# One setup block at the start and the state-space beginning inside the last attention batch of a four-layer conditioned sequence kernel

## The reference, cut to what matters

```python
# L0: 16 heads of 16, gelu MLP (no silu before the modulation)
h = ln(x) * (1 + scale) + shift        # scale, shift = split(cond @ Wln1 + bln1)
x = x + attention(h);  x = x + mlp(ln(x) * (1 + scale2) + shift2)
# L1: 16 heads of 64, L2: 16 heads of 16 with a padding mask; both gated
mod = silu(cond) @ W_mod + b_mod       # shift, scale, gate for attention and for MLP
x = x + gate * attention(modulate(ln(x), ...));  x = x + gate2 * mlp(modulate(ln(x), ...))
# L3: state space in both directions, then a gated MLP
h = ln(x, w, b) * (1 + s1) + sh1
def mamba(h):
    x, z = split(h @ in_proj_W)                    # 512 + 512 channels
    x = silu(causal_conv4(x) + conv_b)
    dt, B, C = from(x @ x_proj_W)                  # dt = softplus(... @ dt_proj_W + dt_proj_b)
    hst = hst * exp(dt * A) + dt * B * x           # 32 states per channel, 512 steps
    return (sum(hst * C) + Dp * x) * silu(z) @ out_proj_W
x = x + g1 * (mamba(h) + flip(mamba(flip(h))))
x = x + g2 * (silu(h2 @ w1) * (h2 @ w2)) @ w3
```

## Time and profile before

| | us |
|---|---|
| runs | 6488.37, 6493.69, 6502.44 |
| median | 6493.69 |
| profiled execution, its own time | 6495.14 |
| its span in the trace | 6493.1 |

### The profile page before, as it was taken

How to read it: one execution, slowest core, us unless ns; L and a number is a source line. 1 busy time by engine, 2 the same in 40 slices (tenths; PEclk the granted TensorE clock), 3 DMA queues, 4 the chain that set the end, 5 groups by cost and what they waited for, 6 DMA issues and landing times. The chain is left out here.

```text
span 6493.1 us, 77727 instructions
## 1 busy us (share of the span) xinstructions
PE 5849.5 (90%) x28624; PEld 3037.7 (47%) x28624; DVE 4492.7 (69%) x4945; ACT 4210.7 (65%) x6876; POOL 2659.1 (41%) x1962
## 2 busy tenths in 40 slices
PE   6989899999999998998997888989899888888887
PEld 3444445555555554444443444444444444444444
DVE  4565663344444345656654898989899898989897
ACT  2444344444555443443443998989898998989896
POOL 0000002222222222000000695959597795959596
PEclk8999999999999999999998999999999999999999
DMA  4221320000000001223131101010110201011100
GB/s 113 51 39 32 58 49 22 1 1 1 1 1 1 1 1 37 50 39 55 32 57 24 53 27 50 30 47 30 42 33 19 58 25 52 30 47 30 47 30 18
DMA packets 152634, 216.11 MB, mean 33 GB/s; under 512 B 24193, under 2 KB 91033, under 8 KB 151745
## 3 DMA queue, kind: packets, MB, share of 16 engines
q1 hardware_dynamic: 152112, 211.08, 14.0%
q10 hardware_dynamic: 144, 0.07, 0.0%
HBM read 146.54 MB, written 30.44 MB: 27 GB/s over the span
## 5 line engine op out<-in xcount | busy, mean ns | idle before, releaser
L2192 DVE TENSOR_TENSOR_SCAN l__h<-l__decay,psum 128x1024 f32<-128x1024 f32 x1024 | 2276.9, 2271 | 74.2 <-ACT l__decay L1800 29.2
L2176 POOL TENSOR_TENSOR l__hc<-l__h,l__c_rep 128x1024 f32<-128x1024 f32 x1024 | 2037.9, 2003 | 186.9 <-DVE l__h L2192 140.4
L1807 PEld LDWEIGHTS psum<-ident,l__dtx_B 128*128 128x128 f32 x8192 | 889.7, 142 | 1102.8 <-DVE l__h L2192 684.9
L1807 PE MATMUL psum<-ident,l__dtx_B 128*128 128x128 f32 x8192 | 1129.9, 282 | 260.7 <-ACT l__dtx_B L1785 185.0
L1800 ACT ACTIVATE l__decay<-l__dt_rep,l__a_neg 128x511 f32<-128x511 f32 x2048 | 1353.4, 712 | 14.9 <-DVE l__h L2192 14.8
L1785 ACT ACTIVATE l__dtx_B<-l__dtx_T,l__b_T 128x512 f32<-128x512 f32 x1792 | 1197.9, 713 | 37.9 <-PEq L2285 35.8
L2261 PE MATMUL psum<-l__hc,l__gather 128*64 128x512 f32 x4096 | 1112.6, 622 | 12.3 <-POOL l__hc L2176 11.7
L192 POOL TENSOR_SCALAR l__ln_var_eps<-l__ln_mean_var 128x4 f32<-128x4 f32 x64 | 17.5, 274 | 2292.2 <-DVE l__ln_mean_var L178 2291.6
L657 DVE TENSOR_REDUCE l__row_max<-psum 128x1 f32<-128x512 f32 x1024 | 658.4, 687 | 250.0 <-PE psum L672 248.8
L1294 POOL TENSOR_SCALAR l__probs<-l__probs,l__rec 128x512 f32<-128x512 f32 x512 | 349.9, 696 | 967.9 <-DVE l__rec L1290 967.8
L966 ACT ACTIVATE l__probs<-psum 128x1024 f32<-128x1024 f32 x512 | 515.6, 1025 | 280.1 <-PE psum L1027 275.7
(11 more groups left out here) (165 smaller groups left out, 6973.1 us busy)
## 6 DMA issues: line engine op xcount, KB each, us to landing
l__c_rep<-l__c_dram SPq DMA_DIRECT2D x512, 128.0 KB, 2.8
l__dt_rep<-l__dt SPq DMA_DIRECT2D x128, 256.0 KB, 4.8
l__parts_dram<-l__parts SPq DMA_DIRECT2D x64, 384.0 KB, 3.8
l__q_stack<-l__parts_dram SPq DMA_DIRECT2D x192, 128.0 KB, 6.4
l__k_stack<-l__parts_dram SPq DMA_DIRECT2D x192, 128.0 KB, 9.1
l__w<-in_l_w SPq DMA_DIRECT2D x6, 1024.0 KB, 7.5
mod_w<-in_mod_w SPq DMA_DIRECT2D x2, 2816.0 KB, 12.5
x_sb<-in_x SPq DMA_DIRECT2D x1, 4096.0 KB, 27.2
```

The lines of the kernel that those rows point to most:

```text
L1807: last = nc.tensor.transpose(bx_psum(i)[:, s, t * P:(t + 1) * P], dtx_B[:, k % 2, t, 2 * c + s, :, :].rearrange("p j d -> p (j d)"), ident ...
L2176: nc.gpsimd.tensor_tensor(hc[:, i % HCS, :, :], h[:, i % HS, :, :], c_of_i, ALU.mult).then_inc(S["hc"], 1)
L2192: nc.vector.tensor_tensor_scan(both(h[:, i % HS, :, :]), both(decay[:, i % DECAYS, :, :]), both(bx_psum(i)), 0.0, ALU.mult, ALU.add).then_ ...
```

## The change

**At the start.** The setup is a class, `Modulation`, and its work stands in the same block as L0's beginning, `alone(setup)`, so one block and one barrier are gone. The columns are in two parts: FIRST (0 to 7, 1024 columns of weights) and REST (8 to 43, 4608). `x` comes in three DMAs: batch 0, batch 1, batches 2 to 7. The mask rows are written, and waited for, after all loads are issued, and L0's stack DMAs (`first_sync`) stand behind that wait on SP.

**At the beginning of L3.** `mamba_layer` returns a `First` and a body. `body2(first3)` hosts batch 0's beginning in L2's last batch, and two blocks (weights, beginning) are gone. ACT takes the four in-projected columns (`take_x`) ahead of `l__hT_mlp`; DVE does the taps (`convolve`) during the MLP; PE projects four of eight in-columns behind the out projection and the rest after the last residual. The memsets of `xproj` and `dtw` are on POOL, `l__a_neg` is made in two steps on ACT. `wout`, `w1`, `w2` and `w3` are loaded in the first batch's block of L3 (`late_sync`). L3's tiles are placed by hand at other addresses (`REGIONS3`), and the two halves of `l__dtx_B` change places. The barrier after L2's last batch clears 120 semaphores where it cleared 60.

```diff
-        alone0()
+        alone0(setup)
         body0(first1)
         body1(first2)
-        body2(None)
+        body2(first3)
+        body3()
 
# alone(setup): sync, vector (parts), tensor
+                    setup.load_first(sp)
                     load(sp)
+                    setup.load_rest(sp)
+                    setup.masks_out(sp)
                     first_sync(sp)
...
-                    ahead.vector(nc, dve, 0, 0)
+                    dve.wait_ge(setup.s_x[0], 16)
+                    norm.stats(nc, dve, ahead.of(0), 0)
+                    setup.mask_rows(dve)
+                    setup.first_columns(dve)
+                    ahead.take_columns(nc, dve, 0)
+                    ahead.scaled(nc, dve, 0, 0)
                     first_vector_stats(dve)
                     first_vector_scaled(dve)
+                    dve.wait_ge(setup.s_x[1], 16)
                     second_vector(dve)
                     first_vector_down(dve)
+                    setup.rest_columns(dve)
+                    dve.wait_ge(setup.s_x[2], 16)
...
+                    for m in setup.FIRST:
+                        setup.fill(pe, m)
+                    pe.wait_ge(setup.s_consts, 4)
                     norm.tensor(nc, pe, 0, bank[0:DC])
                     first_tensor_project(pe)
                     first_tensor_norm(pe)
                     second_tensor(pe)
+                    rest = iter(setup.REST)
+                    for _ in range(len(setup.REST) - LEAD // 3):
+                        setup.fill(pe, next(rest))
                     first_tensor_down(pe)
                     for n in range(LEAD):
                         first_tensor_step(pe, n)
+                        if n % 3 == 2:
+                            setup.fill(pe, next(rest))
                     first_tensor_end(pe)
...
# Modulation.load_first / load_rest / masks_out
+        self.load_w(sp, 0)
+        self.load_x(sp, 0)
+        sp.dma_start(self.bias[:, :], self.io["mod_b"]).then_inc(self.s_in, 16)
+        sp.dma_start(self.nw[:, :], self.io["norm_w"]).then_inc(self.s_in, 16)
+        sp.dma_start(self.nb[:, :], self.io["norm_b"]).then_inc(self.s_in, 16)
+        sp.dma_start(self.m8[:, :], self.io["mask"]).then_inc(self.s_mask_in, 16)
...
+        self.load_x(sp, 1)
+        self.load_w(sp, 1)
+        self.load_x(sp, 2)
# mamba_layer
+        FIRST_BANKS = (7, 6, 0, 1)
+        def first_sync(sp):
+            sp.dma_start(dtb[:, :], io[tag + "dtb"]).then_inc(S["load_a"], 16)
+            sp.dma_start(dp[:, :], io[tag + "dp"]).then_inc(S["load_a"], 16)
+            sp.dma_start(a_neg[:, :, :, :].rearrange("p g c s -> p (g c s)"), io[tag + "alog"]).then_inc(S["load_a"], 16)
+            between_sync(sp)
+        def first_tensor_project(pe):
+            pe.wait_ge(S["load"], 16 * LOADS)
+            pe.wait_ge(S["hT"], DC)
+            for m in range(IC):
+                project_in(pe, m, FIRST_BANKS)
+        first = First(
+            S=S, load=load, sync=first_sync, rstd=lambda pool: norm.gpsimd(nc, pool, 0),
...
+            gpsimd_begin=zero_gpsimd, gpsimd_heads=pads, gpsimd=lambda pool: between_gpsimd(pool, False, True),
+            tensor_project=first_tensor_project, tensor_end=lambda pe: between_tensor(pe, False, True),
+            vector_down=convolve, vector_end=first_vector_end,
+            scalar_heads=lambda act: take_x(act, FIRST_BANKS), scalar_end=first_scalar_end)
...
+                            if k == 2 and b == 0:
+                                late_sync(sp)
```

More of the change, by code:

```diff
@@ L108 @@
     shift: int
+    gpsimd_begin: object = nothing
     gpsimd_heads: object = nothing
@@ L792, in narrow_attention_layer, with alone @@
             scalar_up=second_scalar, scalar_end=nothing)
-        def alone():
+        def alone(setup):
             with nc.Block() as block:
@@ L803, in _ @@
                 def _(pool):
+                    setup.constants(pool)
                     norm.gpsimd(nc, pool, 0)
@@ L1671, in split @@
         return w, g, c
-    with ExitStack() as ctx:
-        def sb(name, shape, dt, where=ctx):
-            return where.enter_context(nc.sbuf_tensor(f"{tag}_{name}", shape, dt))
+    if True:
+        sb = Arena(nc, tag, regions)
         win = sb("win", [P, DC, 2 * DI], FP32)
@@ new lines, in mamba_layer, with late_sync, gather_columns, negative_a @@
+        LOADS = 9
+        def late_sync(sp):
+            for to, of in ((wout, "wout"), (w1, "w1"), (w2, "w2"), (w3, "w3")):
+                sp.dma_start(to[:, :, :], io[tag + of].rearrange("(c p) n -> p c n", p=P)).then_inc(S["late"], 16)
+        def gather_columns(dve):
+            for k in range(2):
+                nc.vector.tensor_copy(gather[half(k), :], ident[half(k), half(k)]).then_inc(S["gather"], 1)
+        def negative_a(act):
+            act.wait_ge(S["load_a"], 48)
+            nc.scalar.activation(a_neg[:, :, :, :], a_neg[:, :, :, :], ACT.Exp).then_inc(S["a_neg"], 1)
+            act.wait_ge(S["a_neg"], 1)
+            nc.scalar.activation(a_neg[:, :, :, :], a_neg[:, :, :, :], ACT.Copy, scale=-1.0).then_inc(S["a_neg"], 1)
+            act.wait_ge(S["a_neg"], 2)
@@ L1840, in between_gpsimd, with convolve @@
                 scale_last(0)
+        def convolve(dve):
+            dve.wait_ge(S["pads"], 2)
+            for c in range(IC):
+                for j in range(1, TAPS):
+                    for w in range(2):
+                        if j == 1:
+                            dve.wait_ge(S["tap0"], 2 * c + w + 1)
+                        else:
+                            dve.wait_ge(S["taps"], 2 * ((TAPS - 1) * c + j - 2) + w + 1)
+                        src = xp[:, c, j:j + T] if w == 0 else xp[:, c, T + 2 * PAD - 1 - j:2 * PAD - 1 - j:-1]
+                        nc.vector.scalar_tensor_tensor(xs[:, c, w, :], src, cw[:, c, j:j + 1], xs[:, c, w, :],
+                                                       ALU.mult, ALU.add).then_inc(S["taps"], 1)
         def between_vector(dve, x_end, nxt, combine_last):
             end, begin = x_end is not None, nxt < B
-            if begin and not end:
-                ahead.vector(nc, dve, nxt, 0)
             if end:
@@ L1988, in between_scalar @@
             if begin:
+                if not end:
+                    negative_a(act)
                 for i in range(DECAYED):
@@ L2289 @@
+        return first, body
 _INPUTS = {
```

687 lines of the change are left out of this document (331 added, 356 removed).

## The result

| | before | after |
|---|---|---|
| median of the runs, us | 6493.11 (4 runs, 6488.37 to 6502.44) | 6444.66 (4 runs, 6441.90 to 6451.02) |
| ratio, 95% interval | | 0.9923, 0.9910 to 0.9937 |
| profiled execution, span | 6493.1 | 6449.2 |

48.5 us faster; 6437.6 was forecast and 6423 to 6452 was the range. Timed again later beside other kernels, the same program took 6436.10 (4 runs) against 6493.07 (15 runs of before), 57.0 faster, ratio 0.9916 (0.9903 to 0.9930).

A forecast was written before the change was run, and what follows sets the result against it. PE works in nearly every slice, so savings must come from stretches where everybody waits for one chain: the start (−23.6) and the way into the state space (−32.45), together −56.05, giving 6437.6 us, range 6423 to 6452.

The forecast's parts named there:

- A: Way into the state space: last residual to fourth x projection shrinks from 45.4 to 9.8 us, −35.6.
- B: L2's last batch: hosting the norm in the score loop costs +4.4 us, bounds 2.8 and 6.1.
- C: L2's last batch: `take_x` ahead of `l__hT_mlp` on ACT costs +0.7 us, bounds 0 and 1.5.
- D: MLP's up projection: idle filled by 16 records, so 14.00 instead of 17.05 us, −3.05, or nothing.
- E: Before L3's decays: `l__a_neg` in line on ACT costs +0.75 us.
- F: Barrier after L2's last batch: clearing 120 semaphores costs +0.35 us, bounds 0 and 1.
- the start's chain: Setup and L0's beginning in one block: maxima's transposes at 88.4 instead of 112.05, −23.6 us, bounds −15 to −38.
- the sign that the prediction had set for being wrong: L3's eight untouched batches change by more than 3 us between the first scan and the end.
- rival 2: Seam gives less: hosting 6.1, up projection stays 17.05, first in projections at low clock (3.5 more); 6447 us, chance 0.18.
- the interleaved columns: L0's scores at the start: four records after every third score, 6.9 us of work, taken as 4.0 added.
- Rival 1: Start's REST columns run at full clock, 12 us instead of 24.0, interleaved ones about 3 less; 6423 us, chance 0.12.
- Rival 4: L3's activations slow at new tile places, each ns costing 3.84 us; 20 ns gives 6514 us; chance 0.05.

The follow-up runs named there:

- the nine columns: Changed kernel with nine REST columns ahead of batch 1's transposes, L2's gate matmuls four steps later and two spare matmuls: 6401.79 against 6493.07, ratio 0.9864.

## Why the prediction was right, and where it was not

| step | forecast | measured |
|---|---|---|
| transposes of batch 1 end | 45.9 | 45.2 |
| 28 columns | 24.0 | 23.9 |
| scores with 8 columns to the maxima | 18.5 | 16.65 |
| start in all | −23.6 | −26.7 |
| A, residual to fourth x projection (45.4) | −35.6 | −36.0 |
| B, hosting | +4.4 | +7.1 |
| C, `take_x` ahead of `l__hT_mlp` | +0.7 | +0.4 |
| D, up projection | −3.05 | −0.4 |
| E and F, to the first scan | +1.1 | +0.7 |
| state-space half | −32.45 | −28.1 |
| L3's batches, first scan to the end | 0 | +10.7 in the first profile, +0.8 and +0.9 in the two later ones of the same program |

The two large terms, the start's chain and A, were read off durations and came within 3.1 and 0.4 us. The misses in the two halves, 3.1 more and 4.35 less, cancelled for the most part: −54.8 where −56.05 was forecast. That is luck, and so is part of the first measurement: with L3's 10.7 in it the sign that the prediction had set for being wrong came true, and only later profiles of the same program (+0.8, +0.9) show that the change does not bring it. Nor does the time alone choose between the forecast and rival 2. The first measurement, 48.5, lies nearer to rival 2's 46.7, the second, 57.0, to the forecast's 56.05.

The start. The loads took as long as the estimate had them; PE's first column began at 9.1 and not 8, which costs nothing, since POOL's memset is later. The step that was off was the interleaved columns: I put 4.0 on top of the 14.5 of 24 scores, they cost 2.1. The reading behind it was wrong, too: I took PE to set the pace of the scores, because it was busy 6.48 of 7.00. In the kernel before, DVE's row maxima ran without a gap, and from the fifth score on each weight load waited for one:

```profile
98.14 14.84 DVE L657 TENSOR_REDUCE l__row_max<-psum 128x1 f32<-128x512 f32 x24 [9.01 <-PE psum L672]
...
100.08 0.10 PEld L672 LDWEIGHTS psum<-l__k_stack,l__q_stack 96*128 96x128 bf16 x1 [0.49 <-DVE l__row_max L657]
```

So the columns went in part into time that PE spent waiting. After the change 21 row maxima again take 13.77 without a gap, 0.66 each (0.62 before), and three scores with four records came every 1.95 us. SP was held to 26.9, not 35, so the stacks had even more room. Rival 1 did not come about here: by the rows, 112 records at 0.213. Its condition failed, since the clock fell in the 6.75 us without work between the projections and the transposes, before the columns. But what I took for the shape's own limit fell with the nine columns at 0.113: the columns did not raise the clock, and they used it where they found it. By the rule of the Trainium skill ("TensorE: Matmul & The Clock Gate", "What's actually happening") a PE kept busy is let up to the full clock; the trace of the kernel with spare wide matmuls has it busy for 48 us at 0.50, so here the rule does not hold.

B was sized by comparing a batch with a guest in L0 and one without in L2. L0 has no gates, so the comparison could not show that gates and guest want the same bank. Hosting without the collision was even cheaper than forecast (2.7). The wait, 2.5, and the clock behind it made up the rest. Two of rival 2's three conditions came about, for other reasons than its own: hosting cost 7.1 (it had 6.1), and the up projection stayed slow (16.69, it had 17.05). The third did not, the 16 records of the in projection took 7.03.

D failed as a step. The forecast said that the 8.20 of idleness would be filled by 7.0 of in projections and the clock stay up. They filled it. What was late next was the copy of `l__hT_mlp`, held by `take_x` on ACT (C in another dress): 2.17 without work right in front of the up projection, 1.34 a little earlier, and the clock fell. The experiment with spare matmuls shows that filling the later gap is enough to keep it.

Rival 4 shows a mistake in the price. I multiplied a record's duration by the number of records. In the profile with 844 ns and in those with 707, ACT works through a unit's instructions at the same pace to 0.2%: 295.9 and 295.4 for a batch's scans. The records of ACT overlap: from one start to the next lie 613 and 612 ns in the median. So this pitch is what counts, and not the duration.

## What to carry to other kernels

A beginning that runs alone between two barriers is priced well by the chain of its rows. Hosting it elsewhere gives most of that back (28.1 of the 36.0 that went away here), if each buffer and bank it brings is checked against those of the host, above all where the host has steps that the model batch lacks. After such a move look for gaps of about 2 us in front of long matmul stretches, since the half clock behind one can cost more than the gap (2.7 for the up projection), and look at the host's other batches: moving one constant by four steps gave 25 to 29 us, about half of what the whole change gave. Before explaining a difference inside the untouched part of a program, profile the same program twice. Before saying which engine paces a loop, look at what each of its instructions waits for, and not at the busy share.

## What the runs showed that was not expected

- Gaps of 2 to 3 us on PE were followed by windows at 0.50 to 0.8 of the clock: behind the gate matmuls (2.50) and in front of the up projection (2.17, and 1.34 before that; 16.69 instead of 14.00).
- Matmuls 8 columns wide ran at 0.113 us a record with the clock at 1.00 and 0.214 at 0.50; at 0.50 they did not raise it in 24 us, nor did columns mixed with 512-wide fp32 ones in 48 us.
- One execution of the changed kernel had the 3840 decays and scalings of L3 recorded at 844 and 839 ns in the median instead of 707 to 713, at a cost of 0.47 us in 295.
- The length of an L3 batch, 360.9 to 364.1 us, went with the granted clock around the end of its scans, in all 91 batches.
- A one-line move of four matmuls in L2 gave 16.4 us in the kernel before and 24 by the batches' lengths in the changed one (17.1 in the seven that host no next layer, 7.0 in the one that does).
